# Cross attention: VectorE masks three of the four score banks of the next step ahead of its copy of turned weights, where it masked two

## The reference, cut to what matters

```python
q, k, v = split(x @ Wq), split(x @ Wk), split(x @ Wv)
q, k = rope(q), rope(k)
scores = q @ k.T / sqrt(16) + attention_mask
w = softmax(scores)
out = w @ v
a_scores = tanh(gate) * softmax(q @ a_k.T / sqrt(16))
out = out + a_scores @ a_v
x = layernorm(x + merge(out) @ Wo)
```

## Time and profile before

| | |
|---|---|
| median of 3 runs | 2833.77 us (2829.94 to 2834.28) |
| the profiled execution | 2829.21 us |
| span in its profile | 2827.4 us |
| mean granted TensorE clock | 0.985 of full speed |
| TensorE busy | 2703.8 us (96%) |
| VectorE busy | 1783.5 us (63%) |
| ScalarE busy | 1342.6 us (47%) |
| cross attention, 128 steps | about 1697 to 2577 us from the span's start |

### The profile page before, as it was taken

The page is one execution under the profiler, slowest core; times in us unless marked ns, Lnnn a source line. Parts: engine busy times, 40 slices in busy tenths (PEclk is TensorE's granted clock), DMA queues, the critical chain, the costliest instruction groups (busy, mean ns, idle before and its releaser), DMA issues. The chain is left out here.

```text
span 2827.4 us, 80568 instructions
## 1 busy us (share of the span) xinstructions
PE 2703.8 (96%) x34134; PEld 1677.6 (59%) x34134; DVE 1783.5 (63%) x5047; ACT 1342.6 (47%) x3265; POOL 475.6 (17%) x626
## 2 busy tenths in 40 slices
PE   7999999999999999999999889999999999976998
PEld 3565555655556565555655556666666666653566
DVE  5565555655656566565655636777877877785633
ACT  3343343433433334333433317777777777784231
POOL 1111111111111111111111132131131221200120
PEclk9999999999999999999999999999999999998999
DMA  5010110110101101101101100000000000001431
GB/s 187 24 36 13 32 47 8 31 42 20 39 20 32 35 13 32 35 14 31 36 13 31 62 20 13 13 2 13 13 2 13 13 2 13 2 2 69 161 164 67
DMA packets 96773, 99.95 MB, mean 35 GB/s; under 512 B 38176, under 2 KB 84384, under 8 KB 95264
## 3 DMA queue, kind: packets, MB, share of 16 engines
q1 hardware_dynamic: 96256, 94.27, 10.4%
q0 software_dynamic: 160, 0.52, 0.0%
HBM read 89.93 MB, written 4.85 MB: 34 GB/s over the span
## 5 line engine op out<-in xcount | busy, mean ns | idle before, releaser
L200 PE MATMUL dr_p<-x_t,dr_w_g 128*128 128x512 f32 x1536 | 745.8, 612 | 11.0 <-DMA dr_w_g<-in_w_in 7.7
L1252 ACT ACTIVATE xa_probs<-xa_probs,xa_low 128x256 f32<-128x256 f32 x1024 | 425.8, 500 | 5.7 <-DVE xa_low L1423 3.2
L200 PEld LDWEIGHTS dr_p<-x_t,dr_w_g 128*128 128x128 f32 x1536 | 266.8, 191 | 228.4 <-issue 218.5
L1183 PEld LDWEIGHTS xa_t<-ident,xa_probs 128*128 128x128 f32 x2048 | 222.9, 141 | 148.0 <-ACT xa_probs L1252 97.1
L624 DVE SCALAR_TENSOR_TENSOR dr_acc<-dr_p,dr_taps,dr_acc 128x510 f32<-128x510 f32 (+2 forms) x384 | 284.9, 742 | 24.9 <-ACT dr_acc L487 17.0
L1183 PE MATMUL xa_t<-ident,xa_probs 128*128 128x128 f32 x2048 | 279.1, 279 | 16.9 <-ACT xa_probs_t L1258 16.9
L1423 DVE CUSTOM_DVE_ANT_0 xa_probs<-xa_s,xa_mask 128x256 f32<-128x256 f32 x512 | 210.6, 411 | 83.4 <-PE xa_s L1165 83.4
L1258 ACT ACTIVATE xa_probs_t<-xa_t 128x512 f32<-128x512 f32 x256 | 152.8, 597 | 184.8 <-PE xa_t L1183 184.5
L1423 DVE CUSTOM_DVE_ANT_0 xa_probs<-xa_s,xa_zeros 128x256 f32<-128x256 f32 x512 | 214.7, 419 | 0.1
L487 ACT ACTIVATE dr_acc<-dr_p,dr_taps 128x512 f32<-128x512 f32 x128 | 87.4, 683 | 236.4 <-PE dr_p L200 236.4
L848 POOL TENSOR_TENSOR dr_first<-dr_n_mat,dr_packed 32x256 f32<-32x256 f32 x128 | 92.2, 720 | 505.5 <-DVE dr_n_mat L750 499.9
(11 more groups left out here) (303 smaller groups left out, 4718.8 us busy)
## 6 DMA issues: line engine op xcount, KB each, us to landing
dr_alpha<-alpha_rows SPq DMA_DIRECT2D x64, 254.0 KB
dr_w_g<-in_w_in SPq DMA_DIRECT2D x48, 256.0 KB, 5.9
dr_alpha<-alpha_rows SPq DMA_DIRECT2D x32, 256.0 KB
ff_wide<-in_fw_qkv SPq DMA_DIRECT2D x8, 1024.0 KB, 14.7
x_t<-in_x_t SPq DMA_DIRECT2D x4, 1024.0 KB, 7.1
tokens<-in_x_tok SPq DMA_DIRECT2D x1, 4096.0 KB, 15.9
dr_wo_g<-in_w_out SPq DMA_DIRECT2D x8, 512.0 KB, 3.7
xa_ctx_b<-in_ctx_t SPq DMA_DIRECT2D x8, 512.0 KB, 3.7
```

The source lines that it names most:

```text
L200: mm = pe.matmul(bank[:, :], w_g[:, k, m, :], x_t[:, k, 2 * S * batch:2 * S * (batch + 1)], start=(k == 0), stop=(k == KC - 1))
L1183: mm = pe.transpose(bank_t[i % 2][:, at:at + P], probs[:, v % 3, i, kind, kt * P:(kt + 1) * P], ident)
L1252: op = act.activation(at, at, ACT.Exp, bias=low[:, v % 3, i, kind:kind + 1], scale=-1.0)
```

## The change

VectorE masks banks 1 and 2 of the next step ahead of the copy, and bank 3 behind it. Before, it masked bank 1 ahead, and banks 2 and 3 behind. No instruction is added or taken away.

```diff
@@ -1447,10 +1447,10 @@
                 if ended(u, 0):
                     dve_take(dve, ended(u, 0))
                 if u + 1 < LAST:
-                    tops(u + 1, 1)
+                    tops(u + 1, 1, 2)
                 copy(u)
                 if u + 1 < LAST:
-                    tops(u + 1, 2, 3)
+                    tops(u + 1, 3)
                 if ended(u, 1):
                     dve_take(dve, ended(u, 1))
                 if u and u % 2 == 0:
```

## The result

The changed kernel takes 2835.80 us, median of 22 runs (2831.19 to 2840.16); the kernel before takes 2831.41 in 22 runs beside it (2826.76 to 2835.35). The ratio is 1.0016, with a 95% interval of 1.0010 to 1.0022: 4.5 us slower (2.8 to 6.2). That is a real slowdown, clear of the noise, and it is small: its middle lies within the 0.2% (5.7 us) that I had called no change.

The account below looks back on a forecast made before the run. TensorE was taken to bound the attention. Losses of 9.7 us less gains of 2.8 made 6.9 us slower, added to the median 2833.77 for 2840.7 us; range 2832.5 to 2843.5.

Parts of the forecast that it names:

- loss 1: Steps 4, 5, 10, 11 of batches 0 to 6: copy a whole pair later; 3.4 us in even steps, 2.0 in odd.
- loss 2: Steps 0 and 8 of batches 2 to 6: weighing later by 0.36 and 0.12 us, 1.8 and 0.6 in all.
- loss 3: Last batch, where no piece covers the weighing in most steps: later weighings lose 1.9 us in sum.
- gain: Scores behind the weighing, mostly in the last batch: last bank masked 0.68 us earlier, so their hold goes; 2.8 us gained.
- rival of the hidden start: Weighing's start-up hides under a streaming projection, so the covered steps lose nothing: -0.9 us, 2832.9; chance 0.17.
- The half clock: Last batch, step 8: its longer stop brings one more stretch at 1.2 GHz; 8.4 us slower, 2842.2; chance 0.15.
- signs of being wrong: Weighings of steps 4 and 5 keep their distance, L1165 stays at 1.28 and 1.39, or another half-clock stretch comes.
- wait of L1432: VectorE's wait ahead of the copy: to drop from 83.3 to some 30 us, in far fewer steps.
- my own case: The whole kernel 6.9 us slower, 2840.7 us; chance 0.54, of it 0.16 within 0.2% and 0.38 beyond.

Follow-up runs that it names:

- waits in another order: Changed kernel with TensorE's waits ahead of the weighing turned round, those for the copies last; ratio 1.0019 against the kernel before, +5.4 us.
- copy ahead of everything: Kernel before with the copy moved ahead of the masking of banks 1, 2 and 3; ratio 1.0068, +19.2 us.
- covered steps alone: Kernel before, bank 2 masked ahead of the copy only in steps 4, 5, 10, 11 of batches 0 to 6; ratio 1.0009, +2.6 us.
- where a wait covers it: Kernel before, bank 2 ahead of the copy only in steps 1, 3, 6, 7, 9, 13, 15 and the last batch's odd steps; ratio 0.9985.
- last batch alone: Kernel before, bank 2 masked ahead of the copy in the last batch only; ratio 0.9994, -1.7 us.
- covered by a wait, better waits: Bank 2 ahead in steps 1, 3, 6, 7, 9, 13, 15 and last batch's odd steps, copies' waits last, against the kernel before; 2825.13 us, ratio 0.9971.

## Why the prediction was right and wrong

The direction and the mechanism were right, the size was 2.4 us too large, and the range held the time: forecast 2840.7, measured 2835.8.

| term | forecast | traced |
|---|---|---|
| loss 1, even steps | 14 x 0.24 = 3.4 | 0.24 to 0.25, one 0.41 |
| loss 1, odd steps | 14 x 0.14 = 2.0 | 0.13 to 0.14 |
| loss 2, step 0 | 0.36 | 0.31 |
| loss 2, step 8 | 0.12 | 0.16 |
| loss 3, step 8 | 0.69, a stop of 1.8 | 0.68, a stop of 1.81 |
| loss 3, step 0 | 0.5 | 0.44 |
| loss 3, even steps 2, 4, 12 | a stop longer by 0.15 each | by 0.32 to 0.35 each |
| step 9 | gains 0.14 by its scores | shorter by 0.68 |
| loss 3, step 10 | 0.25 | 0.00 |
| gain, odd scores | 0.25 each | 0.25 each |
| gain, step 0's scores | 0.07 | 0.07 |

- **Loss 1** holds. "I use 0.15 and 0.26 also where TensorE is not idle" was the choice on which it stood, and against which the rival of the hidden start was set. The weighings start 0.14 and 0.25 behind their copies under a projection too. The one step of 0.41 is step 10 of batch 0.
- **Loss 2** holds with one of its numbers off. The lead left was 0.26 (forecast 0.25) and the copy 0.43 late (forecast 0.44), but at step 0 the weighing follows its copy by 0.20 to 0.21. It has a fourth and a fifth wait, yet it does not cost more than an even step, but less; the experiment with the waits in another order brings it to 0.15. Why it is not more than 0.26 is open.
- **The gain** holds, as costed from the copy's start and the masking's end; the copy ahead of everything shows the same hold growing by a pair.
- **What this leaves.** In batches 0 to 6 the forecast terms come to about 7.1 (7.8 of losses 1 and 2, less 0.35 for step 0's scores and the gains of batch 0), and the trace has 7.06. With the last batch at -0.2 that made 6.9.
- **Loss 3** came near by luck: its errors are of opposite sign. I took off the 0.25 of the odd scores and left the next copy where it was. In steps 2, 4 and 12 VectorE is late next, and the gain of the odd step is not cashed: some 0.2 three times. And the whole pair of step 8 was counted as lost, which ScalarE's work in step 9 hides: 0.5. Nor did step 10 lose the 0.25 that it was to take back. My estimate is that without the clock the order brings -0.56 in this batch, where the forecast terms have some -0.2. It takes steps 1 and 11 against the batch without a slow stretch: -0.14 for step 11, as traced, and -0.19 for step 1, as the scores of step 0 take 1.33 there and could take 1.14; no execution shows that one.
- **The half clock.** The rival was "One stretch more costs about 1.5", at the stop of step 8, with a chance of 0.15, and another stretch in the batch was one of my signs of being wrong. It came in two of four executions of the changed kernel, at that place, and it costs 3.0: two stretches, behind step 8 and behind step 10. It is no property of the order alone, since the same order also ran without.
- **The wait of L1432** fell to 39.2, not to "some 30"; the 55 waits that are left are those longer than a pair and the steps in which a lead brought a new one.

**What stays uneven is traced against measured.** The attention of the eight traces is longer by 8.5 us in the mean (874.9 against 866.3; half of the changed ones have the 3 us of the half clock), the measurement has 4.5 (2.8 to 6.2). The rest would have to lie ahead of the attention, in instructions that are the same in both kernels. There the four executions of the changed kernel took 1.6 us less in the mean, with 6 us between the fastest and the slowest of one kernel, so that this can be chance. The same sign, or next to no difference, shows in the other kernels, all against the same first trace. That the first trace of the kernel before was too short an attention was my last theory, and its further executions speak against it.

The granted clocks of the runs say more. In the runs of one kernel a mean clock lower by 0.001 goes with 1.7 us more, and the kernels drew different clocks. The last column is my estimate, from all runs with a clock on record, of the difference at equal clock:

| | mean clock | measured | attention, traced | at equal clock |
|---|---|---|---|---|
| kernel before (27 and 17 runs) | 0.9839 and 0.9841 | | | |
| covered steps alone | 0.9853 | +2.6 | +2.7 | +5.9 |
| where a wait covers it | 0.9848 | -4.3 | -3.6 | -2.5 |
| waits in another order | 0.9830 | +5.4 | +6.1 | +4.2 |
| copy ahead of all three | 0.9856 | +19.2 | +21.0 | +24.4 |
| last batch alone | 0.9846 | -1.7 | +2.6 | -1.1 |
| covered by a wait, better waits | 0.9856 | -8.2 | -3.7 | -4.3 |
| the changed kernel | 0.9844 | +4.5 | +6.5 | +5.8 |

Each estimate holds to 0.9 to 1.9 us. The first row of experiments is the clearest: its attention has no slow stretch, its 28 steps lost 5.4 us in the trace, and at equal clock it has 5.9. So part of the gap between measured and traced is clock, most of it outside the attention. This is a correlation. The clocks of the 22 runs of the kernel before beside the result are not on record, so that the 5.8 is taken against its 44 runs from the experiments, and what is left remains open.

**What failed** besides the sizes in the table is the base. "The median of the runs shown is 4.6 above it, so I add to the median": that median was of three runs, and with 22 it is 2831.4, 2.4 lower. Half of the miss of 4.9 us comes from there. And of the 0.54 for my own case I put 0.38 beyond 0.2%, though 6.9 lies only 1.2 above the 5.7 that this is; the time of a kernel was known no better than that. For the rules that I weighed: the order of the waits shows the 0.11 us for a fourth wait directly. The Trainium skill, Advanced Engine Details and Errata, Miscellaneous Facts, gives 50 to 100 ns for a semaphore's reading; the trace has somewhat more, and decides.

## What to carry over

A wait on an engine that is not the bound is room only in the steps in which it stands right ahead of the thing that the bounding engine needs: look it up step by step, and move work in front of a hand-over only there. The same edit lost 4.5 us where it was made in every step (7 in the traces of batches 0 to 6), and won 4.3 (1.7 to 6.8) where it was made only in the steps with a wait to fill. On the receiving engine, put the wait that is met last at the end of its list: in the traces it gave back 2.6 us of the 7, though a measured gain is not shown. And forecast from the profiled execution's own time or a median of many runs, not of three.

## What the runs showed that I had not expected

- **A wait that is long met costs 0.11 us on TensorE when it stands behind the blocking one.** 0.25 against 0.14 behind the copy, and 0.14 with the waits turned round. This is for a fourth wait; with a fifth, in step 0, it was 0.20 to 0.24 in all. In a few even steps it was 0.29, once 0.43.
- **The clock falls or does not behind the same stop.** A stop of 2.68 us was followed by a weighing of 1.88 us in the kernel before and of 1.08 with the change in the covered steps alone; 1.81 by 1.08 and by 1.65 in one and the same kernel. The stop's length does not decide it by itself, though it may have a part: at step 0 of the last batch all six executions with a stop of 3.06 to 3.38 us had 6.8 us at 1.2 GHz, and the eight with 2.36 to 2.69 had 3.4 or none. The stretches at 1.2 GHz are nearly all that differs between executions of one attention: 6.8 or 13.7 us of the last batch in the changed kernel, worth 3 us, which is most of what the whole change was about.
- **The part that the change does not touch varies most.** Ahead of the attention the eight executions took 1707.0 to 1713.9 us, while 112 steps of the attention repeat to 0.1. It goes with the clock, though not in strict order: over the fourteen traces the time at 1.2 GHz in this part runs from 44.4 us (1706.5 and 1708.2) to 68.3 us (1717.3). And of the 22 runs of the changed kernel the eleven with a mean clock of 0.985 or 0.986 have a median of 2833.4 us, the eleven with 0.983 or 0.984 one of 2839.1. Effects of a tenth of a microsecond can be read from one trace each, and their sum only from many runs.
